# Each block's results scattered by GpSimd to its tokens' rows, read back plainly; table of extra blocks early, fixed biases added where read

## The reference, cut to what matters

```
logits = xt @ router_w + router_b
scores = softmax(logits) + router_bias
...                                       # the 2 best groups of 4, then idx: 2 experts of each token
gate   = zeros((T, E)).at[arange(T)[:, None], idx].add(vals)
for w1, b1, w2, b2, w3, b3, ge in experts:             # E = 16, D = 512, inner width 128
    h = silu(xt @ w1 + b1) * (xt @ w2 + b2)
    y = y + ge[:, None] * (h @ w3 + b3)
z = silu(xt @ sw1 + sb1) * (xt @ sw2 + sb2) @ sw3 + sb3
x = x + y + z
```

## Time and profile before

| | |
|---|---|
| median of 3 executions | 782.44 us (780.93 to 783.16) |
| profiled execution, its own time | 780.68 us |
| its span, first to last instruction | 778.5 us |
| PE busy | 639.4 us (82%) |
| DVE busy | 615.0 us (79%) |
| ACT busy | 499.8 us (64%) |
| POOL busy | 395.5 us (51%) |

### The profile page before, as it was taken

How to read it: one execution, slowest core, us unless ns; L and a number is a source line. 1 busy time by engine, 2 the same in 40 slices (tenths; PEclk the granted TensorE clock), 3 DMA queues, 4 the chain that set the end, 5 groups by cost and what they waited for, 6 DMA issues and landing times.

```text
span 778.5 us, 12706 instructions
## 1 busy us (share of the span) xinstructions
PE 639.4 (82%) x3455; PEld 315.1 (40%) x3456; DVE 615.0 (79%) x1341; ACT 499.8 (64%) x986; POOL 395.5 (51%) x493
## 2 busy tenths in 40 slices
PE   0597989764485986999999999999999978586870
PEld 0243434321132442444444444444444435274650
DVE  5898888888998686888888888888888868667523
ACT  4666767679476346877778777777777855345330
POOL 1987977969576363554445544455444521400004
PEclk9999999976798998999999999999999999789995
DMA  9566775544245146587756776667664490899755
GB/s 353 181 218 189 145 174 132 113 94 82 57 89 133 60 148 113 145 202 161 183 138 143 159 162 149 142 142 159 124 138 88 91 223 15 274 263 294 185 149 162
DMA packets 231547, 120.11 MB, mean 154 GB/s; under 512 B 214209, under 2 KB 214465, under 8 KB 228562
## 3 DMA queue, kind: packets, MB, share of 16 engines
q1 hardware_dynamic: 230226, 115.42, 60.4%
q0 software_dynamic: 1280, 4.20, 1.7%
HBM read 51.94 MB, written 15.20 MB: 86 GB/s over the span
## 4 chain that ended last, share of the span: by engine, by line
PE 57%; DVE 18%; issue 8%; POOL 7%; DMA 5%; ACT 4%; SPq 1%; POOLq 0%; ACTq 0%; DVEq 0%
PE ps L1150 18%; PE ps L1152 18%; PE ps L1151 17%; DVE arena L1527 5%; DVE arena L1530 4%; ACT arena L807 3%; POOL arena L600 2%; DMA arena<-in_moe_w 2%; PE ps L1318 2%; POOL arena L592 2%; DMA arena<-arena 1%; DVE arena L1524 1%; DVE ss L1677 1%; DVE arena L1765 1%; SPq L477 1%
## 5 line engine op out<-in xcount | busy, mean ns | idle before, releaser
L1150 PE MATMUL ps<-arena 128*128 128x512 f16 (+3 forms) x1019 | 358.9, 357 | 63.8 <-DVE arena L1530 21.3
L1151 PE MATMUL ps<-arena 128*128 128x512 f16 (+3 forms) x1019 | 358.0, 356 | 0.0
L1152 PE MATMUL ps<-arena 128*128 128x512 f16 (+3 forms) x1019 | 356.9, 356 | 0.0
L807 ACT ACTIVATE arena<-arena 128x512 f16<-128x512 f32 (+9 forms) x276 | 174.1, 661 | 60.6 <-DMA arena<-in_moe_w 16.5
L1150 PEld LDWEIGHTS ps<-arena 128*128 128x128 f16 (+1 forms) x1019 | 102.2, 100 | 174.7 <-issue 60.0
L1152 PEld LDWEIGHTS ps<-arena 128*128 128x128 f16 (+1 forms) x1019 | 102.4, 100 | 101.1 <-issue 9.0
L1151 PEld LDWEIGHTS ps<-arena 128*128 128x128 f16 (+1 forms) x1019 | 102.3, 100 | 91.8 <-issue 7.4
L1029 ACT ACTIVATE arena<-arena,mneg 128x512 f32<-128x512 f32 x124 | 88.5, 715 | 34.0 <-DVE mneg L1850 34.0
L736 POOL TENSOR_TENSOR rk<-ss,nh 128x4 f32<-128x4 f32 x32 | 32.6, 1018 | 146.9 <-DVE ss L1527 146.8
L1530 DVE SCALAR_TENSOR_TENSOR arena<-arena,rsp 128x512 f16<-128x512 f32 x128 | 94.9, 798 | 0.0
L807 ACT ACTIVATE arena<-ps 128x512 f16<-128x512 f32 (+2 forms) x105 | 58.8, 586 | 44.8 <-PE ps L1152 31.4
(11 more groups left out here) (156 smaller groups left out, 769.2 us busy)
## 6 DMA issues: line engine op xcount, KB each, us to landing
arena<-in_moe_w SPq DMA_DIRECT2D x18, 768.0 KB, 5.7
arena<-in_ffn_w SPq DMA_DIRECT2D x33, 256.0 KB, 2.9
arena<-in_wq SPq DMA_DIRECT2D x8, 1024.0 KB, 5.1
arena<-in_wo SPq DMA_DIRECT2D x8, 1024.0 KB, 5.2
xs_d<-arena SPq DMA_DIRECT2D x23, 256.0 KB, 5.0
y_d<-arena SPq DMA_DIRECT2D x23, 256.0 KB, 2.7
arena<-in_kv_w SPq DMA_DIRECT2D x4, 1024.0 KB, 6.4
arena<-arena SPq DMA_TRANSPOSE x177, 3.3
```

The lines of the kernel that those rows point to most:

```text
L807: return a.activation(out_, in_, ACT.Copy, scale=scale, bias=bias)
L1150: pe.matmul(out_, lhs[0], rhs[0], start=first, stop=False)
L1151: pe.matmul(out_, lhs[0], rhs[1], start=False, stop=False)
L1152: return pe.matmul(out_, lhs[1], rhs[0], start=False, stop=last)
```

## The change

The results go from the three buffers by an indirect transfer of GpSimd (`result_rows`) to rows of their own: row 1 + 512 j + n for choice j of token n; rows of a block that no token fills go to rows behind these. The target of each row of each block (`target`, 128 x 23) is worked out before the blocks: `tokens_of_rows` (DVE) marks for each token and choice the place in its block and the block, 8 matmuls of PE bring the token's number to its place, and `targets` (DVE) makes row numbers of them; PE waits for this only ahead of block 3, whose bank it uses. At the end each token tile is read with one plain transfer of 512 KB, two from SP and two from ACT. The tables of the extra blocks are made by DVE ahead of block 0. For the 16 fixed blocks the two bias matmuls are gone: ACT's sigmoid and DVE's two operations add the bias from `mb` and `mbs` as they read the bank; the 7 extra blocks keep theirs.

```diff
-        yg = [carve(8 + 2 * i, (D,)) for i in range(2 * NT)]
+        yg = [carve(8 + 4 * i, (2, D)) for i in range(NT)]
...
-        y_d = nc.dram_tensor("y_d", (ROWS, D), F32, kind="Internal").ap()
+        y_d = nc.dram_tensor("y_d", (2 * TOK + 1 + ROWS, D), F32, kind="Internal").ap()
+
+        of_token = y_d[1:2 * TOK + 1].rearrange("(j t p) d -> p j t d", j=2, t=NT)
...
-            def y_store(i):
-                sp.wait_ge(t_ev, i + 1)
-                sp.dma_start(y_d[i * P:(i + 1) * P], yb[i % YB]).then_inc(y_st[i % YB], 16)
-
...
-                if i >= 3:
-                    y_store(i - 3)
-            for i in range(TILES - XB - 3, TILES):
-                y_store(i)
+            for i in range(YB):
+                sp.wait_ge(y_st[i], 16 * ((TILES - 1 - i) // YB + 1))
+            for t in range(0, NT, 2):
+                sp.dma_start(yg[t], of_token[:, :, t]).then_inc(yg_in[t], 16)
...
             rstd(7, 2, 3)
+            g.wait_ge(a_o, HK * NT)
+            g.iota(along, [[1, P]], base=0, channel_multiplier=0).then_inc(const_g, 1)
+            g.iota(token, [[P, NT], [TOK, 2]], base=1, channel_multiplier=1).then_inc(const_g, 1)
             rstd(8, 3, 4)
...
-            for i in range(YB):
-                g.wait_ge(y_st[i], 16 * ((TILES - 1 - i) // YB + 1))
-            for t in range(NT):
-                for j in range(2):
-                    g.indirect_dma_start(yg[2 * t + j], None, y_d, bass.IndirectOffsetOnAxis(places[:, t, j:j + 1], 0),
-                                         bounds_check=ROWS - 1, oob_is_err=False).then_inc(yg_in[t], 16)
+            def result_rows(i):
+                g.wait_ge(t_ev, i + 1)
+                g.indirect_dma_start(y_d, bass.IndirectOffsetOnAxis(target[:, i:i + 1], 0), yb[i % YB], None,
+                                     bounds_check=2 * TOK + ROWS, oob_is_err=False).then_inc(y_st[i % YB], 16)
+
+            g.wait_ge(r_slot, 2)
+            for i in range(TILES):
+                result_rows(i)
...
-                a.activation(sgx[:, i % 2], bank(i % HB)[:, 0:P], ACT.Sigmoid, scale=1.0 / SXW).then_inc(m_sg, 1)
+                if i < NE:
+                    a.activation(sgx[:, i % 2], bank(i % HB)[:, 0:P], ACT.Sigmoid, bias=mb[:, 0, i + NS:i + NS + 1],
+                                 scale=1.0 / SXW).then_inc(m_sg, 1)
+                else:
+                    a.activation(sgx[:, i % 2], bank(i % HB)[:, 0:P], ACT.Sigmoid, scale=1.0 / SXW).then_inc(m_sg, 1)
...
+            for i in range(YB):
+                a.wait_ge(y_st[i], 16 * ((TILES - 1 - i) // YB + 1))
+            for t in range(1, NT, 2):
+                a.dma_start(yg[t], of_token[:, :, t]).then_inc(yg_in[t], 16)
...
+                if i == 3:
+                    pe.wait_ge(r_slot, 2)
...
-                    one_hot = pick[:, i:i + 1] if i < NE else pick_x[:, i - NE:i - NE + 1]
-                    mm = pe.matmul(dst, bias_t[:, part_], one_hot.broadcast_to([P, P]), start=False, stop=True)
+                    if i >= NE:
+                        one_hot = pick_x[:, i - NE:i - NE + 1]
+                        mm = pe.matmul(dst, bias_t[:, part_], one_hot.broadcast_to([P, P]), start=False, stop=True)
...
+            pe.wait_ge(r_oh, 3)
+            pe.wait_ge(m_v, 2)
+            for n in range(2 * NT):
+                mm = pe.matmul(bank(3)[:, 0:TILES], at_slot[:, n], of_block[:, n], start=n == 0, stop=n == 2 * NT - 1)
+            mm.then_inc(r_rank, 1)
...
+            def tokens_of_rows():
+                v.wait_ge(const_g, 6)
+                at_place = places[:, :, :].rearrange("p a b -> p (a b)")
+                own.link(ts(blk_i, at_place, 1.0 / P, ALU.mult, -(P - 1) / (2.0 * P), ALU.add))
+                own.link(v.tensor_copy(blk, blk_i))
+                own.link(stt(in_block, blk, -float(P), at_place, ALU.mult, ALU.add))
+                own.mark(tt(at_slot, along.unsqueeze(1).broadcast_to([P, 2 * NT, P]), wide(in_block, P), ALU.is_equal))
+                own.link(tt(of_block, along[:, 0:TILES].unsqueeze(1).broadcast_to([P, 2 * NT, TILES]), wide(blk, TILES), ALU.is_equal))
+                tt(of_block, of_block, wide(token, TILES), ALU.mult).then_inc(r_oh, 1)
+
+            def targets():
+                v.wait_ge(r_rank, 3)
+                own.link(ts(in_block[:, 0:1], token[:, 0:1], float(2 * TOK), ALU.add))
+                own.link(stt(unused, along[:, 0:TILES], float(P), in_block[:, 0:1].broadcast_to([P, TILES]), ALU.mult, ALU.add))
+                own.link(stt(spare, bank(3)[:, 0:TILES], 0.5, unused, ALU.is_lt, ALU.mult))
+                tt(target, bank(3)[:, 0:TILES], spare, ALU.add).then_inc(r_slot, 1)
+
             def tile_gate(i):
                 v.wait_ge(m_sg, NS + i + 1)
...
+                if i < NE:
+                    stt(hux[:, i % 2], dst[:, 0:P], mbs[:, 0, n:n + 1], sgx[:, i % 2], ALU.add, ALU.mult).then_inc(m_u, 1)
+                    v.wait_ge(m_u, n + 1)
+                    stt(hvx[:, i % 2], dst[:, P:2 * P], mbs[:, 1, n:n + 1], hux[:, i % 2], ALU.add, ALU.mult).then_inc(m_v, 1)
...
-            tables = {11: extra_tiles, 12: extra_weights}
+            tokens_of_rows()
+            extra_tiles()
+            extra_weights()
+            targets()
...
-                if i in tables:
-                    tables[i]()
             for t in range(NT):
-                v.wait_ge(yg_in[t], 32)
+                v.wait_ge(yg_in[t], 16)
```

More of the change, by code:

```diff
@@ L216, in block_kernel @@
         bias_t = carve(125, (2, P), F16)
-        pick = carve(125.5, (NE,), F16)
         pick_x = carve(125.5625, (NE,), F16)
@@ L233, in block_kernel @@
         htx = [carve(39, (2, P), F16), carve(39.5, (2, P), F16)]
-        yg = [carve(8 + 2 * i, (D,)) for i in range(2 * NT)]
+        yg = [carve(8 + 4 * i, (2, D)) for i in range(NT)]
+        at_slot, of_block = carve(10, (2 * NT, P), F16), carve(12, (2 * NT, TILES), F16)
+        along, token = carve(12.5, (P,), I32), carve(13, (2 * NT,), I32)
+        blk_i, in_block, blk = carve(13.0625, (2 * NT,), I32), carve(13.125, (2 * NT,)), carve(13.1875, (2 * NT,))
+        spare, unused, target = carve(13.25, (TILES,)), carve(13.375, (TILES,)), carve(13.5, (TILES,), I32)
         extra_i, began, ended, row = (carve(122, (NE,), I32), carve(122.0625, (NE,)), carve(122.125, (NE,)),
@@ L1481, in tile_hidden @@
                     for k in range(KD):
+                        ends = i < NE and k == KD - 1
                         col = part_ * D + k * P
@@ L1486, in tile_hidden @@
                             lhs = [arena16[:, bass.ds(off + w * 3 * D + col, P)] for w in range(2)]
-                        product(dst, lhs, [xg[i % XB][:, w * KD + k] for w in range(2)], k == 0, False)
-                    one_hot = pick[:, i:i + 1] if i < NE else pick_x[:, i - NE:i - NE + 1]
-                    mm = pe.matmul(dst, bias_t[:, part_], one_hot.broadcast_to([P, P]), start=False, stop=True)
+                        last = product(dst, lhs, [xg[i % XB][:, w * KD + k] for w in range(2)], k == 0, ends)
+                        if ends:
+                            mm = last
+                    if i >= NE:
+                        one_hot = pick_x[:, i - NE:i - NE + 1]
+                        mm = pe.matmul(dst, bias_t[:, part_], one_hot.broadcast_to([P, P]), start=False, stop=True)
                 mm.then_inc(m_h, 1)
@@ L2066, in _ @@
             own.link(tt(pick_f, ident[:, 0:NE], ident[:, 32:32 + NE], ALU.add))
-            own.mark(ts(pick, pick_f, SW, ALU.mult))
             own.link(ts(iota_1, iota, 1.0, ALU.add))
@@ L2091, in extra_weights @@
                 v.tensor_copy(wplace[:, :], xbase).then_inc(rows_ready, 1)
+            def tokens_of_rows():
[13 more added lines that the diff above has]
+                tt(target, bank(3)[:, 0:TILES], spare, ALU.add).then_inc(r_slot, 1)
             def tile_gate(i):
                 v.wait_ge(m_sg, NS + i + 1)
-                tt(hux[:, i % 2], bank(i % HB)[:, 0:P], sgx[:, i % 2], ALU.mult).then_inc(m_u, 1)
-                v.wait_ge(m_u, NS + i + 1)
-                tt(hvx[:, i % 2], bank(i % HB)[:, P:2 * P], hux[:, i % 2], ALU.mult).then_inc(m_v, 1)
+                n, dst = i + NS, bank(i % HB)
+                if i < NE:
+                    stt(hux[:, i % 2], dst[:, 0:P], mbs[:, 0, n:n + 1], sgx[:, i % 2], ALU.add, ALU.mult).then_inc(m_u, 1)
+                    v.wait_ge(m_u, n + 1)
+                    stt(hvx[:, i % 2], dst[:, P:2 * P], mbs[:, 1, n:n + 1], hux[:, i % 2], ALU.add, ALU.mult).then_inc(m_v, 1)
+                else:
+                    tt(hux[:, i % 2], dst[:, 0:P], sgx[:, i % 2], ALU.mult).then_inc(m_u, 1)
+                    v.wait_ge(m_u, n + 1)
+                    tt(hvx[:, i % 2], dst[:, P:2 * P], hux[:, i % 2], ALU.mult).then_inc(m_v, 1)
             def tile_low(i):
@@ L2123, in _ @@
                         v.wait_ge(x_sum, 2 * t + 1)
-                    stt(xres[:, t], yg[2 * t + j], gsc[:, t, j:j + 1], xres[:, t], ALU.mult, ALU.add).then_inc(x_sum, 1)
```

(1 more changed line is left out.)

## The result

The changed kernel's median is 775.3 us over seven executions, beside 781.7 us (778.04 to 783.64) of the kernel before on the same chip; one execution of 1135.16 us at less than two thirds of the others' granted clock is left out. The ratio is 0.9919 with a 95% interval of 0.9896 to 0.9942, or 6.3 us less. The profiled execution took 774.98 us, its span is 773.1.

A forecast was written before the change was run, and what follows sets the result against it. Bounds: expert weights from 693 to 714 us, then a table stall, PE from 727 to 755, a transfer chain at the end. -4.5 + 0.5 - 1.5 - 1.2 = -6.7 gave 774.0 us, stated as 774.5; range 772 to 777, chance 0.55.

The forecast's parts named there:

- The chance of 0.84: Whole kernel: chance given to its being faster, the forecast's own case and the two faster rivals together.
- Tables early: PE between out(11) and out(13): wait for DVE's table rows and slow blocks behind it go; -4.5 us, bounds 2.5 and 4.7.
- Their new place: DVE's idle 10.44 us before block 0's gate: the new rows fit, ending at 680.5 with 4 us spare; 0.
- Biases where they are read: Ten blocks that DVE paces: multiplies with a bias cost 0 to 0.06 us more each; +0.5 us, range 0 to 1.2.
- Stores leave SP's queue: 693 to 714 us: weights of experts 15 to 17 go out up to 2 us earlier; -1.5 us, range 0 to -3.8.
- Scatters in the loop: Result buffers in the block loop: scatters land 4.3 us after the copy, within the 5.6 us ACT allows in blocks 11 to 15; 0.
- The end: After block 19's copy: scatters, four plain reads and additions replace 8 gathers; -1.2 us, range -3.8 to +0.6.
- L: Time from a scatter's start to its landing, taken as 3.4 us; paid twice at the end, in fast blocks from 4.7.
- two slower landings in series: At the end: scatters of blocks 19 and 22 land one after the other, taking back most of the gain from dropped gathers.
- More of the same side: Rival: weights come when asked for, -3.8, and scatters land early, -3.5 at the end; about 769.5 us; chance 0.15.
- PE gains only its idle time: Rival: the clock dips elsewhere or ACT's copies hold the fast blocks, so the tables give -2.5; 777.5 us; chance 0.14.
- Slower: the scatters land late: Rival, end and fast blocks: late landings cost the whole gain (chance 0.07) or more, up to 785.5 us (0.09).

The follow-up runs named there:

- experiment 1: Kernel before, with only the two tables of the extra blocks made ahead of block 0; 0.9967, 2.6 us (1.3 to 3.8) less.
- experiment 2: Changed kernel with the tables back at blocks 11 and 12 and all biases added by PE; 0.9961, 3.1 us less than the kernel before.
- Experiment 3: Changed kernel with the bias matmuls of the 16 fixed blocks back on PE; 0.9912 to the kernel before, median 775.31 us.
- experiment 4: Changed kernel with SP waiting for the copy of block i - 3 where the store stood, without storing; 0.9923, median 775.62 us.
- experiment 5: Changed kernel with a fourth result buffer; 0.9915 to the kernel before, median 775.74 us.
- 6: Changed kernel with each token tile's read cut in two halves, one from SP and one from ACT; 0.9877, median 773.14 us.
- 7: Changed kernel with fixed biases back on PE, a fourth result buffer and the reads in halves; 0.9895, median 773.35 us.

## Why the prediction was right, point by point

774.5 us was predicted and 775.3 measured; 6.7 us less was the sum, 6.3 and 8.1 were measured in two comparisons (781.7 to 775.3 by ratio, 782.64 to 774.53 by medians). The chance of 0.84 was on the right side. The path is right: the wait for the table is gone, the front has room, and the end is shorter. That the sum comes so close is in part luck: the tables' term was one to two microseconds too large and the end's one to two too small. The terms, one by one, with the sizes as the traces show them (three of the kernel before, nine with scatters):

- **Tables early, -4.5.** The mechanism is shown: by the first experiment alone and by the pair of the second and third, the tables' place is worth 2.6 (1.3 to 3.8) and 3.6 us. Two blocks take 3.98 us where 4.1 was forecast. The term is too large by one to two microseconds of timed gain. The forecast took the lower clock behind the stall as a fixed part of the price; it is there in three of three traces of before, and absent in the trace of experiment 2, which has the stall too. That it is absent in some of the timed executions of the kernel before would explain why the timed gain is under the traces' 4.1, but their clock by stretch isn't recorded, so this is argued and not shown.
- **Their new place, 0.** Right. The new rows end 22.8 us after `places`, which on the first trace's 657.49 is 680.3, where 680.5 was forecast, and DVE has 4.55 us to spare.
- **Biases where they are read, +0.5.** DVE's price is at the upper bound, 0.12 a block (bounds 0 and 0.12), so 1.2 over ten blocks. Timed, the kernels can't be told apart; an earlier block 0, which the forecast put at nothing, may give it back, which isn't shown. Net the term is some 0.5 too high, within what can be measured.
- **Stores leave SP's queue, -1.5.** The size is about right: block 9's sigmoid comes 57.8 us after `places` in the mean of nine traces with scatters and 58.9 in the mean of four without, 1.1 less, the biases' price included. The weights of the last expert are asked for 3 us earlier and used 1 us earlier: the full transfers take the rest, as the forecast argued. The reason that I had for SP standing still, the wait for a result, was wrong in the main: with the same waits and no stores the last weights go out 0.5 to 1.3 us later than without the waits, but 3.0 us earlier than before, and the time is the same (experiment 4). So it is the stores in SP's queue that cost. Their bytes are still moved, by GpSimd's scatters in the same stretch; whether the issue costs or the place in the queue isn't told apart.
- **Scatters in the loop, 0.** The size is right, but the landing behind it was read wrongly, and that it did no harm is luck. The earlier trace rows holds all transfers of `xs_d`; its 8.1 us is one of SP's transposing reads, and of GpSimd's scatters of tokens that trace has no landing. The trace of experiment 1 has them: 2.7 to 7.5 us, six of the eight over 5.5. The scatters of results are as slow in the loop: in the first trace of the changed kernel those of blocks 1 and 2 took 8.1 and 7.2 us, that of block 10 took 4.67 and that of block 11 at least 5.0, where 3.4 was put in. It fits all the same, because the early blocks are some 3 us apart, and in blocks 11 to 15 ACT's few waits (experiment 4) don't show in the time. GpSimd's own part was foreseen: a scatter costs it 1018 ns in the mean of 23, 0.97 when DVE is idle and at most 1.32. In the first trace of the changed kernel the profile shows no wait of ACT for one until block 21. Where the fixed biases are PE's, scatters of 2.56 us appear (last section), and even these fit: that kernel takes the same time.
- **The end, -1.2.** This step was mis-sized the most: from copy 19 to the end of the span it is 21.4 and 22.2 us in the two traces of the changed kernel, beside 24.2 to 24.4 before, so -2.0 to -3.0; the longer of the two holds the late landing of 4.65. L is 2.8 us instead of 3.4 and enters twice (1.2 in all), the wake 0.77 instead of 0.9 twice (0.3), and the additions take 5.89 instead of 6.2 (0.3). These make the 1.7 between the forecast and the first trace. The reads came after 4.90, as the 5.0 of the earlier trace rows said. The "two slower landings in series" do stand in the chain, but with the wait between them gone only 0.37 us is won (experiment 5): GpSimd's own pace is right behind.

The gather's 3.4 us, from which L was taken, had a landing and the wake of DVE behind it, and a bounds-checked read of scattered rows; it was an upper bound and I took it for the value. The Trainium skill, DMA: Bandwidth & Descriptors, section "Anatomy of one DMA — SWDGE (gpsimd) path", would by its fit give, as an estimate, 2.6 us for 256 KB. In the last seven blocks 2.71 to 2.91 were measured in the first trace of the changed kernel, so the fit was the better guide for L there; for the 4.65, and for the loop's 3 to 8 us beside full transfers, it is not. For the first reads it would give 4.4 against 4.90, and there the row was better; the page's fit is for transfers of GpSimd, and SP and ACT issue these.

**The rivals.** "More of the same side", 769.5, is not what happened, though the end went its way. "PE gains only its idle time" gave 777.5. For the tables alone the timed ratio gives just that, 2.6, though the trace shows the clock's part won too; the whole result is beyond it. "Slower: the scatters land late" is refuted as a time, but its condition came true in part: L is 2.8 in the chain of the end, with 4.65 and 4.63 for block 18 in two traces, and in the loop it passes the 4.7 from which the forecast let the fast blocks pay (4.82 to 6.84 for blocks 10 to 13 in experiment 4). That kernel's median is 775.62 beside 775.3, so the price that the forecast set on it was too high there; why, no run shows.

## What to carry to other kernels

A stall on the bounding engine cost its idle time in each of four traces here, and the lower clock behind it, 1.6 us, came in three of them: put the first into the sum and the second into the range. When small tables can be worked out early, look for an idle stretch of the same engine and add the rows up; the sum here was right within a tenth of the room. A gather at the end, one transfer after another of one engine, can be traded for scatters during the loop when the scattering engine is otherwise idle. Take their landing from transfers beside the same load, and from the right rows: in the loop here it was 3 to 8.6 us, at the quiet end 2.8, so the number of buffers and the pace of the blocks must allow for the first. What remains at the end is one landing, one read and the additions, and reads in halves on two queues bring the first addition earlier.

## What the runs showed that I had not expected

- **The clock after a wait.** In the kernel before PE idles 2.53 us and the granted clock falls from 2.4 to 1.2 GHz for 3.4 us; it idles 2.63 us in experiment 2 and the clock stays up. Nor does it fall in the kernel before behind PE's longer wait of 2.77 us for DVE that ends at 712.93, so the length of one wait doesn't tell it. In the changed kernel it falls elsewhere, behind a wait of 2.88 us for DVE's low half; PE's timeline and the stretch behind it:

```profile
714.07 0.61 PE L1165 MATMUL ps<-arena 128*128 128x512 f16 x1 [2.88 <-DVE arena L1556]
```

```profile
714.10:717.70 3.60, 3.60 (x27) 2.77 (x28) 2.72 (x5) 3.00 (x6) 1.09 (x2) 0.53 1.17 295
```

Such a drop stands in four of the six traces whose fixed biases are off PE. There it costs nothing that can be seen, since DVE and the weights set the pace of those blocks: from block 6's sigmoid to block 9's it is 10.1, 10.1, 10.3 and 10.5 us with the drop, and 10.6 and 9.9 in experiments 5 and 6, whose clock stays up.
- **A late sigmoid.** In six of nine traces with scatters ACT's sigmoid of block 15 starts some 1.8 us after all that it needs seems done; in the changed kernel's timeline of ACT:

```profile
731.51 0.37 ACT L1129 ACTIVATE arena<-ps,mb 128x128 f32<-128x128 f32 x1 [1.82 <-remote]
```

The semaphores' events in the trace tell what it waits for: PE's signal that the hidden product of block 15 is done comes at 731.49, though the product's last matmul is recorded as ended at 729.72, 1.8 us earlier. In experiment 4, one of the three traces without the late sigmoid, the same signal comes 0.01 us after the recorded end. The ends of matmuls are modelled in the profile, so whether the product or only its signal is late, and why, stays open. It costs no time that I can find.
- **A scatter beside a long row of DVE.** In the three traces with plain multiplies in the fixed blocks (experiments 2, 3 and 7) some scatters take 2.56 us, in no other. Experiment 3, timelines of DVE and of GpSimd:

```profile
701.16 1.96 DVE L1549 SCALAR_TENSOR_TENSOR arena<-arena 128x128 f16<-128x128 f32 x2 [0.38 <-ACT arena L815]
```

```profile
701.40 2.56 POOL L804 DMA_INDIRECT y_d<-arena  x1 [26.98 <-ACT arena L815]
704.29 2.56 POOL L804 DMA_INDIRECT y_d<-arena  x1 [0.33 <-issue]
```

and the changed kernel, the same two:

```profile
702.64 1.96 DVE L1556 SCALAR_TENSOR_TENSOR arena<-arena 128x128 f16<-128x128 f32 x2 [0.38 <-ACT arena L814]
```

```profile
702.77 1.02 POOL L803 DMA_INDIRECT y_d<-arena  x1 [2.05 <-ACT arena L814]
```

DVE's row holds a short subtraction and the low half of 1536 columns right behind it. The low half itself starts at 701.36 in the first and at 702.85 in the second. Where the scatter starts 0.04 us after it, it lasts until 703.96, 0.84 us after DVE's row has ended at 703.12; where it starts 0.09 before it, it is done in 1.02. This holds in all nine traces: the 29 scatters that start 0.03 us or more into such a low half all end 0.84 to 0.85 us after its end, whether that makes them 1.32 or 2.56 us long, and the 43 that start earlier beside it take 0.97 to 1.07. So a scatter waits for the long instruction to end, if this one had begun first. The Trainium skill, SBUF — State Buffer, section "SBUF: two separate sides", says that DVE and GpSimd share a pair of ports, that a DVE instruction with two inputs in SBUF contends for it with a GpSimd instruction that reads SBUF, and that whichever starts first holds it for the whole instruction. The low half has two such inputs and the scatter reads its row numbers there, and the trace agrees in this order; in the other order the low half isn't held up, but takes its usual 1.75 us, or 1.82 where both start within 0.03 us. No run takes the long rows away, so that the ports are the cause is argued and not shown. A shift of a tenth of a microsecond between the engines decides over 1.5 us of GpSimd's time, which here nobody waits for.
- **Landings differ.** The scatter of 256 KB took 2.7 to 2.9 us in the last blocks of one execution, 4.65 once in those of another, and up to 8.6 in the first blocks, beside the loads of expert weights.
